# Second attention of a two-layer gated block: the negative maxima leave VectorE as four columns and come back as one row that TensorE reads with a stride

## The chip, the cores and the metric

The kernel runs on one core of a Trainium2 chip. The metric is the device time of one execution in microseconds (us). Engines are named as in the profile: PE is TensorE (PEld its weight loads), DVE VectorE, ACT ScalarE, POOL GpSimd, SP SyncE, which here issues the DMAs. The program is written instruction by instruction: each engine has a queue that it works through in order, and semaphores tie the queues together.

## The reference, cut to what matters

Two layers, each a gated cross attention on a context of 1601 tokens and a gated feed-forward part. The change lies in the second layer's attention:

```python
q = (text_hidden @ Wq).reshape(B, T_text, 16, 128)...      # B = 4, T_text = 256
k = (vision_tokens @ Wk).reshape(B, T_vis, 8, 128)...      # T_vis = 1601
scores = jnp.einsum('bhtd,bhsd->bhts', q, k) / scale
scores = jnp.where(mask, scores, -jnp.inf)
attn = jax.nn.softmax(scores, axis=-1)
out = jnp.einsum('bhts,bhsd->bhtd', attn, v)
return out.transpose(0, 2, 1, 3).reshape(B, T_text, 2048) @ Wo
```

Softmax needs, for each query and head, a number near the maximum of its scores, to be subtracted before the exponential.

## The kernel before, in words

A planner (class `Plan`) writes out lists of pieces: `plan.main` for the first layer and the second attention (`stage0` to `stage2`), `plan.ffn` for the last feed-forward part. Each engine's function (`tensor_main`, `vector_main`, `scalar_main`, `gpsimd_main`, `sync_main`) goes over the same list and issues its share of each piece, so the list sets the order of every queue. What runs at once is decided by the distance between pieces in the list and by the waits.

The second attention (`stage2`) works on 32 groups g: 4 batches by 8 pairs of heads. A group has 512 query columns (2 heads by 256 queries) in `qh` (high half, bf16) and `ql` (low half). The keys come in 13 tiles of up to 128. Scores are computed transposed, keys on partitions and queries along the row. For a tile s = 13 g + kt the pieces are:
- `s1`: PE makes the scores in bank 0 or 1 with three matmuls of 512 columns. For kt 0 and 1 a fourth one goes first (L1389): it adds the row of negative maxima, `mrw`, to each key's scores; its weights are ones, and of `mrw` only partition 0 is not zero. The scores of the tiles from 2 on are taken against key differences (`dch`), so the row needs to be added to two tiles only, since it then stays in the sum. ACT takes the exponential (L1975).
- `c1`: ACT casts it to bf16 (L1982). `r1`: DVE makes the low half (L1719). POOL adds the tiles up for the denominators (L2115, L2118).
- `v1`, three tiles later: three matmuls with the values, into bank 2 or 3; they wait for `r1` of their tile (`p_low`).

After a group: `o1a` (PE, 4 float32 products of one column into bank 7, once POOL has all sums: `summed1`), DVE L1722 and L1724, POOL L2124 makes a diagonal matrix, `o1b` (PE, float32, bank 7) spreads it, ACT copies it (L1998), `o1c` (DVE L1733) scales the output.

Ahead of a group come its queries (`qp`, 12 matmuls, then `ql`) and its maxima: `md` and `mb` (16 matmuls of 512 or 289 columns into banks 4 to 6, ACT L1993, DVE L1700), then `mf`: DVE reduces 128x8 to `mm1`, 128x4 (L1706): partition n, column u holds the maximum of query 128 u + n. Then the columns must become a row:
- `m1n`: PE transposes `mm1` into bank 7 (L1377), DVE clamps and negates the 4x128 result into `mng` (L1711), which frees bank 7.
- `m1r`: SP writes `mng` to DRAM, 4 rows of 128 (L2231), waits for it, and reads the 512 numbers back into partition 0 of `mrw` (L2236).

In the list three other steps of the maxima's generator lie between `mf` and `m1n`, about two tiles; `m1r(g)` comes after s1(13 g - 9), nine tiles ahead of the group's first scores. Bank 7 is shared: `m1n`, `o1a`, `o1b`, the transposes of the normalisation (`ln3`, L1043), output projections. Each of these waits until the one before it in the list has been emptied (`free[7]`). L722 is a helper through which all matmuls but the transposes go, and L658 is the helper that waits. All SBUF tiles lie in one tensor, so the profile calls them `arena`; the banks are `BK`; `rowd` is the DRAM scratch.

Of the kernel before, what the change touches and what calls it, by code (L numbers as in the profile page):

```python
# [6 lines left out]
BF16 = mybir.dt.bfloat16  # L7
U8 = mybir.dt.uint8
I32 = mybir.dt.int32
ALU = mybir.AluOpType  # L10
# [38 lines left out]
class Plan:  # L49
# [424 lines left out]
    def maxima(self, g):  # L474
        for k in range(9):
            if k < 8:
                self.fill(self.turn(g, 4), "md", g, k // 2, k % 2)
                self.main.append(("md", g, k // 2, k % 2))
                yield
            if k:  # L480
                self.fill(self.turn(g, 5), "mb", g, (k - 1) // 2, (k - 1) % 2)
                self.main.append(("mb", g, (k - 1) // 2, (k - 1) % 2))
                yield
        self.main.append(("mf", g))
        yield
        yield
        yield
        self.fill(7, "m1n", g)
        self.main.append(("m1n", g))
        yield  # L490
        self.rowed.add(g)
        self.main.append(("m1r", g))
        yield

    def stage2(self):
# [7 lines left out]
            to.append(p)  # L503

        def masked(b):
            assert b < 2 or ("m1n", 8 * (b - 1) - 1) in self.slot
            assert ("m1n", 8 * b) not in self.slot
            for k in range(7):
                piece("mk", b, k)
                yield  # L510
# [161 lines left out]
def program(nc, a, out):  # L672
    root = ExitStack()
    with root:
# [5 lines left out]
        def sem(name):  # L680
            return root.enter_context(nc.semaphore(name))
# [39 lines left out]
        def mm(out_, lhsT, rhs, start=True, stop=True):  # L721
            return T.matmul(out_, lhsT, rhs, start=start, stop=stop, skip_group_check=True)  # L722
# [129 lines left out]
        on1 = sb("on1", [128, 128], F32, CTb)  # L852
        ones = sb("ones", [128, 128], F32, CTb)
        dn = sb("dn", [128, 8], F32, CTb)
        mng = sb("mng", [4, 2, 128], BF16, CTb)
        Ph = [sb(f"Ph_{i}", [128, 512], BF16, (L1, CTb)[i == 0]) for i in range(NR)]
        Pl = [sb(f"Pl_{i}", [128, 512], BF16, (L1, SM)[i == 0]) for i in range(NR)]
        ckf = sb("ckf", [128, NKT, 128], F32, L1)
# [231 lines left out]
        def pool_mask(b, k):  # L1090
            if k == 6:
# [4 lines left out]
                for lo, hi in ((0, 401), (401, HALF)):  # L1096
# [11 lines left out]
        mcb_done, q_high, max1_done, p_high, p_low, summed1, pv_done, diag_done, ck_high, ck_low, tern_done = (  # L1108
            sem(n) for n in ("mcb_done", "q_high", "max1_done", "p_high", "p_low", "summed1", "pv_done",
                             "diag_done", "ck_high", "ck_low", "tern_done"))  # L1110
        l1_set, t_lt, t_half, dn_recip, pv_taken = (sem(n) for n in ("l1_set", "t_lt", "t_half", "dn_recip", "pv_taken"))

        def prep_over(queue):
# [13 lines left out]
        def tensor_main():  # L1127
            for piece in plan.main:
# [238 lines left out]
                elif kind in ("md", "mb"):  # L1367
# [3 lines left out]
                    pe.wait_ge(mx_ready, g // 8 + 1)  # L1371
                    mm(BK[i][:, 0:hi - lo], qh[:, g % 3, 128 * u:128 * u + 128],
                       (cmd if kind == "md" else cmb)[:, g // 8 % 2, lo:hi]).then_inc(full[i], 1)
                elif kind == "m1n":
                    g, = arg
                    pe.wait_ge(max1_done, g + 1)
                    T.transpose(BK[7][0:4, 0:128], mm1[:, :], idn[:, :]).then_inc(full[7], 1)  # L1377
                elif kind == "s1":
                    s, = arg
                    g, kt = s // NKT, s % NKT  # L1380
                    b, r, m = g // 8, g % 3, rows_of(kt)[0]
                    ks = slice(128 * kt, 128 * kt + m)
                    high = cth[:, b, ks] if kt < 2 else dch[b][:, 128 * kt - 256:128 * kt - 256 + m]
                    o = BK[i][0:m, :]
                    pe.wait_ge(*emptied("qp", g))
                    if kt < 2:
                        pe.wait_ge(rows1[g % 2], 16 * (g // 2 + 1))
                        pe.wait_ge(l1_set, 4)
                        mm(o, onb[:, 0:m], mrw[:, g % 2, :], stop=False)  # L1389
                    mm(o, high, qh[:, r, :], start=False, stop=False)  # L1390
                    mm(o, high, ql[:, r, :], start=False, stop=False)
                    mm(o, ctl[:, b, ks], qh[:, r, :], start=False).then_inc(full[i], 1)
                elif kind == "v1":
                    s, = arg
                    g, kt = s // NKT, s % NKT
                    b, k, m = g // 8, s % NR, rows_of(kt)[0]
                    j = 2 + g % 2
                    pe.wait_ge(p_low, s + 1)
                    pe.wait_ge(ck_low, 3 * b + 3)
                    if kt == 0:  # L1400
                        pe.wait_ge(pv_taken, g - 1)
                    mm(BK[j][:, :], ckh[0:m, b, kt, :], Ph[k][0:m, :], start=(kt == 0), stop=False)
                    mm(BK[j][:, :], ckl[0:m, b, kt, :], Ph[k][0:m, :], start=False, stop=False)
                    mm(BK[j][:, :], ckh[0:m, b, kt, :], Pl[k][0:m, :], start=False,
                       stop=(kt == NKT - 1)).then_inc(pv_done, 1)
                elif kind == "o1a":
                    g, = arg
                    pe.wait_ge(summed1, 12 * (g + 1))
                    pe.wait_ge(l1_set, 4)
                    for u in range(4):  # L1410
                        t = mm(BK[7][:, u:u + 1], acc[:, g % 2, 128 * u:128 * u + 128], ones[:, 0:1])
                    t.then_inc(full[7], 1)
                elif kind == "o1b":
                    g, = arg
                    pe.wait_ge(diag_done, g + 1)
                    mm(BK[7][:, :], ones[:, :], dg[:, :, :].rearrange("p u n -> p (u n)")).then_inc(full[7], 1)
                elif kind == "o1h":
                    t2, = arg
                    i, n = slot["o1p", B - 1, t2]
                    pe.wait_ge(free[i], n)  # L1420
                    pe.wait_ge(pv_taken, 8 * B - 1)
                    project1(i, t2, 0, H - 2)
                elif kind == "o1p":
                    b, t2 = arg
                    pe.wait_ge(pv_taken, 8 * b + 8)
                    project1(i, t2, H - 2 if b == B - 1 else 0, H).then_inc(full[i], 1)
                elif kind == "twc":
                    k, = arg
                    pe.wait_ge(t_half, 3 * k + 1)
                    mm(BK[7][:, 0:1], on1[:, :], asum[:, k:k + 1]).then_inc(full[7], 1)  # L1430
# [13 lines left out]
        def vector_main():  # L1444
# [10 lines left out]
            for piece in plan.main:  # L1455
# [247 lines left out]
                elif kind == "mf":  # L1703
                    g, = arg
                    dve.wait_ge(*emptied("mb", g, 3, 1))
                    V.tensor_reduce(mm1[:, :], mp1[:, :, :], AX.X, ALU.max).then_inc(max1_done, 1)  # L1706
                elif kind == "m1n":
                    g, = arg
                    dve.wait_ge(full[7], n + 1)
                    dve.wait_ge(bounced1[g % 2], 16 * (g // 2))  # L1710
                    V.tensor_scalar(mng[:, g % 2, :], BK[7][0:4, 0:128], -1e20, -1.0, ALU.max, ALU.mult).then_inc(free[7], 1)  # L1711
                elif kind == "r1":
                    s, = arg
                    k, m = s % NR, rows_of(s % NKT)[0]
# [419 lines left out]
        def sync_main():  # L2134
# [13 lines left out]
            for piece in plan.main:  # L2148
# [77 lines left out]
                elif kind == "m1r":  # L2226
                    g, = arg
                    k = g % 2
                    sp.wait_ge(*emptied("m1n", g))
                    sp.wait_ge(rows1[k], 16 * (g // 2))  # L2230
                    SP.dma_start(rowd[k][0:4, :], mng[:, k, :]).then_inc(bounced1[k], 16)  # L2231
                    sp.wait_ge(bounced1[k], 16 * (g // 2 + 1))
                    sp.wait_ge(l1_set, 4)
                    if g >= 2:
# [243 lines left out]
```

## Time and profile before

| | |
|---|---|
| median of 3 runs | 1621.13 us (1619.86 to 1626.16) |
| the profiled execution's own time | 1623.28 us |
| its span | 1622.0 us |
| second attention, from the first transpose of maxima to the last group | about 684 to 1560 us |
| busy over the whole span | PE 87%, DVE 76%, ACT 68%, POOL 50% |

The span is what the profile covers; the execution's time is 1.28 us longer. Busy shares are means over stages that are limited differently, so the chain of waits and the idle time ahead of single instructions are what tells where a removed instruction or wait counts. The busy time of matmuls is modelled at their ends, so the spacing of starts is the better measure of what one costs in a dense stretch. "PEclk" is the granted clock of TensorE as a share of 2.4 GHz.

### The profile page before, as it was taken

Reading aid. Unit: us, or ns where it says so; the run is one execution under the profiler, and the core shown is the slowest. Engines: PE = TensorE matmul, PEld = TensorE weight load, DVE = VectorE, ACT = ScalarE, POOL = GpSimd, SP = SyncE. Lnnn points to the kernel's source line nnn. Section 1 sums busy time; section 2 is a strip of 40 time slices with the busy share of each in tenths; the row PEclk is TensorE's granted clock in tenths of the full one; section 3 lists DMA queues with packets and bytes.
Section 4 is the critical chain, followed back from the end, with each engine's and each line's share of the span. In section 5 each row is a group of like instructions: output and inputs, shape, how many; then the busy total and the mean of one; then the engine's idle time right before and its main releaser. Section 6 shows DMA issues by size and latency. Waiting matters only on the chain.

```text
span 1622.0 us, 25718 instructions
## 1 busy us (share of the span) xinstructions
PE 1412.5 (87%) x8502; PEld 695.3 (43%) x8588; DVE 1233.2 (76%) x2247; ACT 1104.4 (68%) x2028; POOL 805.2 (50%) x664
## 2 busy tenths in 40 slices
PE   5788788888888888788899988899988999899999
PEld 3243243343333343244455544445543446454455
DVE  6667667767786256688999586979689997899857
ACT  4657656756755755487788586778587876787844
POOL 4014013014040022178778468687497875587843
PEclk9798998999988999899999999999999999999999
DMA  4001200300340100100000000000010000000000
GB/s 159 1 1 38 46 2 1 62 2 1 63 183 1 53 1 6 36 27 6 1 1 1 21 1 26 1 2 21 1 27 27 1 27 1 27 1 1 1 1 27
DMA packets 20491, 36.72 MB, mean 23 GB/s; under 512 B 4898, under 2 KB 15238, under 8 KB 19334
## 3 DMA queue, kind: packets, MB, share of 16 engines
q1 hardware_dynamic: 20358, 35.07, 7.4%
q8 instruction: 69, 1.13, 0.3%
q14 instruction: 64, 0.52, 0.1%
HBM read 26.53 MB, written 1.15 MB: 17 GB/s over the span
## 4 chain that ended last, share of the span: by engine, by line
PE 32%; DVE 9%; issue 7%; POOL 7%; ACT 4%; DVEq 0%; ACTq 0%; POOLq 0%
PE BK L722 32%; DVE arena L1719 4%; POOL arena L2118 4%; DVE arena L1700 2%; ACT arena L1982 1%; ACT arena L1975 1%; POOL arena L2124 1%; POOL arena L2115 1%; ACT arena L1993 1%; ACT L1975 0%; DVE arena L2307 0%; POOL arena L2103 0%; POOL arena L2092 0%; DVE arena L1071 0%; DVE arena L2313 0%
## 5 line engine op out<-in xcount | busy, mean ns | idle before, releaser
L722 PE MATMUL BK<-arena 128*128 128x512 bf16 (+11 forms) x8172 | 1366.5, 367 | 174.1 <-DVE arena L1537 39.3
L722 PEld LDWEIGHTS BK<-arena 128*128 128x128 bf16 (+6 forms) x8258 | 659.0, 111 | 852.0 <-issue 213.9
L2118 POOL TENSOR_TENSOR arena<-arena 128x512 f32<-128x512 f32 (+1 forms) x352 | 506.2, 1438 | 155.1 <-ACT arena L1975 132.9
L1719 DVE TENSOR_TENSOR arena<-arena 128x512 bf16<-128x512 f32 (+1 forms) x416 | 498.4, 1206 | 31.6 <-ACT arena L1982 30.4
L1975 ACT ACTIVATE arena<-BK,arena 128x512 f32<-128x512 f32 (+1 forms) x416 | 286.8, 689 | 128.7 <-PE BK L722 112.8
L1873 ACT ACTIVATE arena<-BK 128x512 f32<-128x512 f32 (+1 forms) x416 | 227.3, 604 | 92.7 <-PE BK L722 87.1
L1537 DVE TENSOR_REDUCE arena<-BK 128x1 f32<-128x512 f32 x384 | 244.5, 684 | 59.7 <-PE BK L722 58.6
L1982 ACT CAST arena<-arena 128x512 bf16<-128x512 f32 (+1 forms) x416 | 254.1, 611 | 0.0
L1700 DVE CUSTOM_DVE_ANT_0 arena<-BK,arena 128x512 bf16<-128x512 f32 (+1 forms) x256 | 145.1, 567 | 40.1 <-PE BK L722 39.8
L1993 ACT ACTIVATE arena<-BK 128x512 bf16<-128x512 f32 (+1 forms) x256 | 130.9, 512 | 58.1 <-PE BK L722 56.8
L2029 POOL TENSOR_TENSOR arena<-arena 128x256 f32<-128x256 f32 (+6 forms) x45 | 30.2, 671 | 186.4 <-ACT arena L1810 184.1
L2115 POOL TENSOR_TENSOR arena<-arena 128x512 f32<-128x512 f32 x32 | 45.7, 1430 | 65.0 <-ACT arena L1975 65.0
L2056 POOL TENSOR_TENSOR arena<-arena 128x512 bf16<-128x512 f32 x24 | 28.2, 1173 | 98.6 <-ACT arena L1839 79.6
L1664 DVE TENSOR_TENSOR arena<-BK,arena 128x512 f32<-128x512 f32 x32 | 22.0, 688 | 46.7 <-ACT arena L1929 46.6
L2124 POOL TENSOR_TENSOR arena<-arena 128x512 f32<-128x512 f32 x32 | 47.5, 1484 | 10.5 <-DVE arena L1724 10.5
L1793 ACT COPY arena<-BK 128x256 f32<-128x256 f32 (+1 forms) x52 | 18.9, 372 | 48.0 <-DVE arena L1483 48.0
L1483 DVE TENSOR_TENSOR arena<-BK,arena 128x256 f32<-128x256 f32 (+1 forms) x56 | 23.5, 422 | 36.1 <-PE BK L722 36.1
L2073 POOL CAST arena<-arena 128x256 bf16<-128x256 f32 x16 | 6.4, 398 | 82.2 <-ACT arena L1913 82.2
L2040 POOL TENSOR_TENSOR arena<-arena 128x1024 f32<-128x1024 f32 (+2 forms) x15 | 23.4, 1593 | 29.2 <-DVE arena L974 29.2
L1739 DVE SCALAR_TENSOR_TENSOR arena<-BK,arena 128x256 f32<-128x256 f32 x8 | 3.9, 483 | 42.5 <-PE BK L722 42.5
L1998 ACT COPY arena<-BK 128x512 f32<-128x512 f32 x32 | 18.8, 587 | 25.2 <-PE BK L722 25.2
L2103 POOL TENSOR_TENSOR arena<-arena 128x384 bf16<-128x384 f32 (+1 forms) x20 | 19.9, 1015 | 23.2 <-ACT arena L1953 23.2
(179 smaller groups left out, 876.3 us busy)
## 6 DMA issues: line engine op xcount, KB each, us to landing
arena<-arena SPq DMA_DIRECT2D x144, 50.0 KB, 2.2
arena<-in_ctxT SPq DMA_DIRECT2D x8, 800.5 KB, 4.5
arena<-in_ctxk SPq DMA_DIRECT2D x4, 768.0 KB
arena<-in_wo SPq DMA_DIRECT2D x1, 2048.0 KB, 7.4
arena<-in_wqT SPq DMA_DIRECT2D x1, 2048.0 KB, 7.5
arena<-in_x SPq DMA_DIRECT2D x4, 256.0 KB, 9.8
arena<-in_rsel SPq DMA_DIRECT2D x1, 1024.0 KB, 9.4
arena<-in_rw1T SPq DMA_DIRECT2D x1, 1024.0 KB, 5.2
```

The source lines that it names most:

```text
L722: return T.matmul(out_, lhsT, rhs, start=start, stop=stop, skip_group_check=True)
L1537: V.tensor_reduce(mxp[:, g % 2, u, c:c + 1], BK[i][:, :], AX.X, ALU.max).then_inc(free[i], 1)
L1700: V.tensor_tensor_reduce(out=junk[:, 0:w], in0=BK[i][:, 0:w], in1=rl[:, k % 3, 0:w], scale=1.0, scalar=-3e38, op0=ALU.add, op1=ALU.max, ac ...
L1719: V.tensor_tensor(Pl[k][0:m, :], P1[k][0:m, :], Ph[k][0:m, :], ALU.subtract).then_inc(p_low, 1)
L1873: A.activation(P0[(2 * s + r) % NP][0:m, :], BK[i][0:m, :], ACT.Exp, scale=0.25).then_inc(free[i], 1)
L1975: A.activation(P1[k][0:m, :], BK[i][0:m, :], ACT.Exp, scale=SCALE1, bias=mcb[0:m, b, kt:kt + 1]).then_inc(free[i], 1)
L1982: A.copy(Ph[k][0:m, :], P1[k][0:m, :]).then_inc(p_high, 1)
L1993: A.activation(rl[:, k % 3, 0:w], BK[i][:, 0:w], ACT.Relu).then_inc(free[i], 1)
L2029: G.tensor_tensor(sv[:, :, 0:w], sv[:, :, 0:w], sv[:, :, w:2 * w], ALU.add).then_inc(pool_chain.sem, pool_chain.up())
L2115: G.tensor_tensor(acc[:, g % 2, :], P1[(s - 1) % NR][:, :], P1[k][:, :], ALU.add).then_inc(summed1, 1)
L2118: G.tensor_tensor(acc[0:m, g % 2, :], acc[0:m, g % 2, :], P1[k][0:m, :], ALU.add).then_inc(summed1, 1)
L2124: G.tensor_tensor(dg[:, :, :], idn[:, :].unsqueeze(1).to_broadcast([128, 4, 128]), dn[:, 4:8].unsqueeze(2).to_broadcast([128, 4, 128]), AL ...
```

## The change

The transpose is gone. DVE clamps and negates `mm1` where it lies, right behind the reduction, in piece `mf`; `mng` is now 128 partitions of 4 numbers. The piece `m1n` no longer exists, though the generator yields as often as before, so all other pieces keep their places. A new semaphore, `max1_neg`, tells SP. The store to DRAM moves 128 pieces of 4 bf16 numbers (8 bytes) where it moved 4 of 256 bytes, and number 4 n + u of the DRAM row is now query 128 u + n. It is read back as it lies, so the matmul that adds the row (64 of them, two in each group) reads `mrw` in steps of 4 elements, 8 bytes: 128 elements from offset 0, 128 from offset 1, and so on.

```diff
@@ Plan.maxima
-        self.fill(7, "m1n", g)
-        self.main.append(("m1n", g))
         yield
         self.rowed.add(g)
         self.main.append(("m1r", g))
@@
-        mng = sb("mng", [4, 2, 128], BF16, CTb)
+        mng = sb("mng", [128, 2, 4], BF16, CTb)
@@ tensor_main
-                elif kind == "m1n":
-                    g, = arg
-                    pe.wait_ge(max1_done, g + 1)
-                    T.transpose(BK[7][0:4, 0:128], mm1[:, :], idn[:, :]).then_inc(full[7], 1)
@@ s1
-                        mm(o, onb[:, 0:m], mrw[:, g % 2, :], stop=False)
+                        mm(o, onb[:, 0:m], mrw[:, g % 2, :].rearrange("p (n u) -> p u n", u=4), stop=False)
@@ vector_main
                     V.tensor_reduce(mm1[:, :], mp1[:, :, :], AX.X, ALU.max).then_inc(max1_done, 1)
-                elif kind == "m1n":
-                    g, = arg
-                    dve.wait_ge(full[7], n + 1)
+                    dve.wait_ge(max1_done, g + 1)
                     dve.wait_ge(bounced1[g % 2], 16 * (g // 2))
-                    V.tensor_scalar(mng[:, g % 2, :], BK[7][0:4, 0:128], -1e20, -1.0, ALU.max, ALU.mult).then_inc(free[7], 1)
+                    V.tensor_scalar(mng[:, g % 2, :], mm1[:, :], -1e20, -1.0, ALU.max, ALU.mult).then_inc(max1_neg, 1)
@@ sync_main, m1r
-                    sp.wait_ge(*emptied("m1n", g))
+                    sp.wait_ge(max1_neg, g + 1)
                     sp.wait_ge(rows1[k], 16 * (g // 2))
-                    SP.dma_start(rowd[k][0:4, :], mng[:, k, :]).then_inc(bounced1[k], 16)
+                    SP.dma_start(rowd[k][0:4, :].rearrange("a (b u) -> (a b) u", u=4), mng[:, k, :]).then_inc(bounced1[k], 16)
                     sp.wait_ge(bounced1[k], 16 * (g // 2 + 1))
```

On PE, around the transpose of group 13, this stands in the queue before (the matmuls of 512 columns that wait for `p_low` are `v1`, those that wait for free0 or free1 are `s1`, the 256-column ones `qp`, and the one-column ones `o1a` of group 11):

```order
L722 MATMUL BK<-arena 128x512 [waits free0]
L722 MATMUL BK<-arena 128x512 x2
L1377 MATMUL BK<-arena 4x128 [waits max1_done,free7]
L722 MATMUL BK<-arena 128x512 [waits p_low]
L722 MATMUL BK<-arena 128x512 x2
L722 MATMUL BK<-arena 128x512 [waits free1]
L722 MATMUL BK<-arena 128x512 x2
L722 MATMUL BK<-arena 128x256 [waits free4]
L722 MATMUL BK<-arena 128x256 x11
L722 MATMUL BK<-arena 128x1 [waits summed1,free7]
L722 MATMUL BK<-arena 128x1 x3
L722 MATMUL BK<-arena 128x512 [waits p_low]
```

And this stands at the same place now:

```order
L720 MATMUL BK<-arena 128x512 [waits free0]
L720 MATMUL BK<-arena 128x512 x2
L720 MATMUL BK<-arena 128x512 [waits p_low]
L720 MATMUL BK<-arena 128x512 x2
L720 MATMUL BK<-arena 128x512 [waits free1]
L720 MATMUL BK<-arena 128x512 x2
L720 MATMUL BK<-arena 128x256 [waits free4]
L720 MATMUL BK<-arena 128x256 x11
L720 MATMUL BK<-arena 128x1 [waits summed1,free7]
L720 MATMUL BK<-arena 128x1 x3
L720 MATMUL BK<-arena 128x512 [waits p_low]
```

Only the transpose has gone; but `free7` at `o1a` now stands for an earlier user of bank 7, no longer for the transpose that DVE must have read.

On DVE, for the same group, before (L1719 is `r1`, L1071 to L1079 are the mask of the next batch, L1722 is `o1a`):

```order
L1706 TENSOR_REDUCE arena<-arena 128x4 [waits free5]
L1719 TENSOR_TENSOR arena<-arena 128x512 [waits pv_done,p_high]
L1071 TENSOR_SCALAR arena<-arena 128x1601
L1073 TENSOR_TENSOR arena<-arena 128x2 [waits dve_own]
L1075 TENSOR_SCALAR arena<-arena 128x1 [waits dve_own]
L1077 RECIPROCAL arena<-arena 128x1 [waits dve_own]
L1079 SCALAR_TENSOR_TENSOR arena<-arena 128x1 [waits dve_own]
L1719 TENSOR_TENSOR arena<-arena 128x512 [waits pv_done,p_high]
L1711 TENSOR_SCALAR arena<-BK 4x128 [waits bounced11,full7]
L1719 TENSOR_TENSOR arena<-arena 128x512 [waits pv_done,p_high]
L1722 TENSOR_SCALAR arena<-BK 128x4 [waits full7]
```

Now the clamp stands right behind the reduction (all line numbers are lower by some):

```order
L1701 TENSOR_REDUCE arena<-arena 128x4 [waits free5]
L1704 TENSOR_SCALAR arena<-arena 128x4 [waits bounced11,max1_done]
L1712 TENSOR_TENSOR arena<-arena 128x512 [waits pv_done,p_high]
L1069 TENSOR_SCALAR arena<-arena 128x1601
L1071 TENSOR_TENSOR arena<-arena 128x2 [waits dve_own]
L1073 TENSOR_SCALAR arena<-arena 128x1 [waits dve_own]
L1075 RECIPROCAL arena<-arena 128x1 [waits dve_own]
L1077 SCALAR_TENSOR_TENSOR arena<-arena 128x1 [waits dve_own]
L1712 TENSOR_TENSOR arena<-arena 128x512 [waits pv_done,p_high] x2
L1715 TENSOR_SCALAR arena<-BK 128x4 [waits full7]
```

The clamp moved up over two `r1` (and here over the mask's five instructions), and waits for the reduction on its own engine where it waited for PE. On SP the order of the DMAs is as before.

## Rows read from the trace of the kernel before

**Rows 1.** The page's busy times and its chain by engine.

```profile
PE 1412.5 (87%) x8502; PEld 695.3 (43%) x8588; DVE 1233.2 (76%) x2247; ACT 1104.4 (68%) x2028; POOL 805.2 (50%) x664
...
PE 32%; DVE 9%; issue 7%; POOL 7%; ACT 4%; DVEq 0%; ACTq 0%; POOLq 0%
```

**Rows 2.** Busy time by stretch: us, PE, PEld, DVE, ACT, POOL, PEclk, DMA, GB/s.

```profile
1068.00:1134.00 66.00, 65.39 (x317) 32.44 (x323) 57.90 (x98) 54.61 (x100) 50.20 (x37) 0.97 0.04 13
683.00:1550.00 867.00, 791.70 (x3876) 404.11 (x3948) 738.77 (x1233) 655.17 (x1176) 635.32 (x457) 0.99 0.04 11
```

**Rows 3.** Chain in order of time, pieces on PE's transpose: start, us, what (15 such).

```profile
684.25 0.37 PE BK L1377
...
1495.10 0.11 PE BK L1377
```

**Rows 4.** Timeline of PE around transposes, of a dense stretch and behind it.

```profile
1109.91 0.27 PE L1377 MATMUL BK<-arena 128*4 128x128 f32 x1
1110.10 23.14 PE L722 MATMUL BK<-arena 128*128 128x512 bf16 x116
...
1133.07 0.27 PE L1377 MATMUL BK<-arena 128*4 128x128 f32 x1
...
1173.01 0.27 PE L1377 MATMUL BK<-arena 128*4 128x128 f32 x1
```

**Rows 5.** Timeline of PE, its idle time that ends with DVE L1711 (10 such rows).

```profile
809.15 8.01 PE L722 MATMUL BK<-arena 128*128 128x1 f32 x38 [0.71 <-DVE arena L1711]
...
945.83 0.66 PE L1043 MATMUL BK<-arena 128*128 128x128 f32 x4 [1.05 <-DVE arena L1711]
...
1259.49 3.88 PE L722 MATMUL BK<-arena 128*128 128x1 f32 x20 [0.51 <-DVE arena L1711]
...
1397.35 0.66 PE L1043 MATMUL BK<-arena 128*128 128x128 f32 x4 [2.46 <-DVE arena L1711]
```

**Rows 6.** Timeline of all engines around the longest of them.

```profile
1029.96 0.16 DVE L1706 TENSOR_REDUCE arena<-arena 128x4 f32<-128x8 f32 x1
...
1036.28 0.27 DVE L1711 TENSOR_SCALAR arena<-BK 4x128 bf16<-4x128 f32 x1
...
1036.61 1.08 PE L722 MATMUL BK<-arena 128*128 128x1 f32 x8 [2.55 <-DVE arena L1711]
...
1037.72 0.16 DVE L1722 TENSOR_SCALAR arena<-BK 128x4 f32<-128x4 f32 x1 [0.57 <-PE BK L722]
...
1037.92 0.18 DVE L1724 RECIPROCAL arena<-arena 128x4 f32<-128x4 f32 x1
...
1037.93 4.24 PE L722 MATMUL BK<-arena 128*128 128x512 bf16 x12 [0.24 <-issue]
```

**Rows 7.** Busy time by stretch, behind two of the stalls (columns as in Rows 2).

```profile
1037.00:1041.00 4.00, 3.76 (x14) 1.79 (x16) 2.83 (x6) 0.69 (x2) 1.41 (x1) 0.57 0.00 1
1041.00:1044.00 3.00, 3.00 (x14) 1.38 (x13) 2.14 (x2) 2.52 (x5) 2.52 (x2) 1.00 0.00 0
945.00:949.00 4.00, 3.12 (x26) 2.68 (x28) 2.20 (x3) 3.10 (x6) 2.44 (x3) 1.00 0.00 1
```

**Rows 8.** Chain in order of time, pieces on DVE L1711 (8 such).

```profile
1308.31 0.21 DVE arena L1711
```

**Rows 9.** Groups of instructions by form, 680 to 1550 us: count, busy us and mean ns.

```profile
L722 PE MATMUL BK<-arena 128*128 128x512 bf16 x2522 | 610.6, 382 | 46.8 <-DVE arena L1719 35.0 <-ACT arena L1975 4.9 <-ACT arena L1993 1.3
...
L722 PE MATMUL BK<-arena 128*128 128x512 f32 x62 | 34.2, 635 | 16.3 <-POOL arena L2124 16.3
```

**Rows 10.** DMA issues: two on SP in time; two small ones, KB, us to landing.

```profile
1111.94 0.24 SPq L2231 DMA_DIRECT2D rowd<-arena  x1
...
1113.08 0.21 SPq L2236 DMA_DIRECT2D arena<-rowd  x1
...
rowd<-arena SPq DMA_DIRECT2D x16, 4.0 KB, 1.4
...
arena<-in_mcol SPq DMA_DIRECT2D x1, 6.0 KB, 4.2
```

More of the change, by code:

```diff
@@ L505, in masked @@
         def masked(b):
-            assert b < 2 or ("m1n", 8 * (b - 1) - 1) in self.slot
-            assert ("m1n", 8 * b) not in self.slot
+            assert b < 2 or 8 * (b - 1) - 1 in self.rowed
+            assert 8 * b not in self.rowed
             for k in range(7):
@@ L1110, in program @@
                              "diag_done", "ck_high", "ck_low", "tern_done"))
+        max1_neg = sem("max1_neg")
         l1_set, t_lt, t_half, dn_recip, pv_taken = (sem(n) for n in ("l1_set", "t_lt", "t_half", "dn_recip", "pv_taken"))
```

## The prediction

> **What bounds the kernel now.** I read the page first. Over the whole span PE is busy 87% and is the largest part of the chain that ended last, but a third only, with DVE and POOL behind it [rows 1]; the reader is to see that no engine is the bound throughout. So I went to the stage of the change. From 683 to 1550 us PE is busy 792 of 867 us and DVE 739 [rows 2]. In a dense stretch such as 1068 to 1134 us PE is busy 65.4 of 66 us: there a group takes 23.16 us, one transpose to the next, and every PE instruction counts. The next group takes 39.9 us [rows 4]; the mean of the stage is 867/32 = 27 us, and in the slower groups the chain runs over DVE or POOL for long pieces. A PE instruction is therefore worth its time only where the chain passes through it; for the transpose that is so 15 times of 32 [rows 3].
>
> Then I looked for the idle time of PE that the removed instructions end. There are ten such places, of 0.40 to 2.55 us [rows 5, 6]. Their cause is in the order, not in the transpose's own length: bank 7, which the next piece needs (`o1a` seven times, a normalisation's transpose three times), is freed by DVE L1711, and L1711 stands on DVE behind an `r1` (L1719). When DVE is late, PE stands before a bank although it has work that needs nothing of it. Eight of these ten are on the chain [rows 8]; those at 1259 and 1520 us are not, where POOL leads.
>
> **What is removed on PE.** 32 transposes. In the dense stretch the next matmul starts 0.19 us after the transpose [rows 4], so one costs about 0.2 us of PE, 6.4 us in all, and on the chain 15 x 0.2 = 3.0 us. The other 17 fall into time in which PE would wait anyway.
>
> **What the freed bank gives.** After the stall, PE did the blocked piece (1.08 us for `o1a` [rows 6], 0.66 us for the normalisation's four transposes [rows 5]) and then `v1`, which needs the `r1` that stood just ahead of L1711. Without L1711 the blocked piece runs inside the stall, and PE then waits for the end of that `r1`, which lies 0.27 + 0.04 us before the old release. So each place on the chain gives the smaller of its stall and 0.31 us plus the piece: 0.71 twice (809 us and one like it), 0.97 for the normalisation's three (stalls 1.05, 1.05, 2.46), 0.51 twice (like that at 1259 us), and 1.39 for the stall of 2.55. That is 1.42 + 2.91 + 1.02 + 1.39 = 6.7 us.
>
> The longest place has something on top. PE stood 2.55 us, and behind it the granted clock was 0.57 over 4 us, mostly the lower level of 1.2 GHz, and 2.4 GHz (1.00) after that [rows 7]; the twelve matmuls from 1037.93 took 4.24 us [rows 6]. At full clock 116 starts take 22.97 us (1110.10 to 1133.07 [rows 4]), 0.20 us each with shorter ones among them, so 0.21 for one of 512 columns and 2.5 us for twelve. With `o1a` run inside it, the wait shrinks to some 1.2 us. Behind the idle of 1.05 us at 945.83 PE kept its full clock [rows 7], so I take the loss as gone: 1.7 us. If it is not, that term is nothing.
>
> **DVE.** L1711 took 0.27 us on 4x128 from PSUM. The new instruction is 128x4 from SBUF, nearest to L1722, 128x4 from PSUM, 0.16 us [rows 6]. Its wait for the reduction on its own engine is like that of L1724 behind L1722, which starts 0.04 us after its end [rows 6]. I bound the pair with its wait between 0.04 us more than L1711 alone (0.31) and, as that is the smallest row here, 0.07 us less (0.16 + 0.04); taken: the latter, 2.2 us of DVE time, of which a tenth or so is on the chain, 0.2 us. It now delays the `r1` behind the reduction by 0.2 us, and spares the one behind the old place 0.27 us, so nothing is late next.
>
> **The DMAs.** SP issues the read of the row 1.14 us after the write [rows 10]; that is the write's whole way. The new write has 128 pieces of 8 bytes instead of 4 of 256. Bounds: the same 1.1 us, or 4.2 us as the small load over 128 partitions, 3.1 us more. The write of the first layer's maxima, 16 pieces, lands in 1.4 us [rows 10], and the queues are as good as idle, so I take some 1.5 us. What hides it: `m1r(g)` stands nine tiles before the group's first scores, and a tile takes 23.1/13 = 1.8 us, so 16 us are there even in the dense stretch. SP's queue has DMAs of context and mask behind it, needed later still. The clamp's earlier place (at 1030.2 and no longer 1036.3 [rows 6]) adds cover. Only group 0 has no nine tiles: its chain goes reduction, transpose, clamp, two DMAs. Its transpose is on the chain with 0.37 us [rows 3] and is counted; at the upper bound this one place would lose about 2 us. Taken: 0.
>
> **The strided read.** 64 matmuls read the same 512 columns of the same type, with a step of 8 bytes. No row shows a strided moving operand. It can't be faster than contiguous, so the lower bound is 0. The upper bound I take from the nearest slower reading, the float32 product of 512 columns: 34.2 us for 31 products, 1.10 us each, against 610.6/2522 = 0.24 us [rows 9]; 0.86 us more, 55 us over 64 matmuls. The row it is nearest to is the bf16 one, which differs in nothing but the step; taken: 0.
>
> The Trainium skill, "SBUF — State Buffer", section "Door 1: The DMA port swizzle", has a note on lines of 16 bytes. It says two or more hits in a line reach full bandwidth, by which a step of 8 bytes costs nothing; the same note says that each access that crosses to a new line pays a penalty, and this read crosses at every second element where the contiguous one crosses at every eighth. By the first half the sum stands; by the second it is the rival below. No run here shows which.
>
> **The sum.** 3.0 + 6.7 + 1.7 + 0.2 + 0 + 0 = 11.6 us on the chain of before. It is not all kept: a chain that lay just behind takes over. DVE is busy 85% and POOL 73% of the stage [rows 2], and every place where PE was held by DVE's lateness is one where DVE is the next bound, since v1 and the exponentials go on depending on it. I keep two thirds: 8 us. Against the profiled execution's own 1623.3 us this gives 1615.3; that execution is 2.2 us above the median of 1621.1, so for a median 1613.
>
> **Rivals.**
> - *The strided read runs at half rate.* A length more, 0.21 us, 64 x 0.21 = 13.4 us of PE. By the share of the transposes, 15 of 32 are on the chain, and a little more as PE gets longer: 7 us. It eats the gain: 1620. For it: nothing in the trace speaks against it, and the second half of the note; against it: the first half.
> - *The strided read runs at a quarter rate or worse, and the kernel is slower.* Three lengths more, 0.63 us per matmul, 40 us of PE; at this size PE becomes the bound in more groups, and I take 0.6 of it, 24 us, less the gain of 8: 1637. The point from which this mechanism makes the kernel slower by more than 8 us is (8 + 8)/(64 x 0.6) = 0.4 us per matmul, about three times its length. For it: float32 products are four to five times as long as bf16 ones [rows 9]. Against it: those do more passes; this one has the same columns.
> - *The stalls move and nothing is gained.* PE gets past bank 7 and waits for the same DVE `r1` at `v1`; chains of POOL and DVE take back all but the transposes in the dense groups: 3 us kept at most, 1618 to 1621. For it: the two idle places off the chain, and groups that POOL leads. Against it: in the dense groups nothing is close behind PE.
> - *The new DMA is late.* It would have to take 16 us, except for group 0; 2 us there, and a median of 1615. The trace gives it little.
>
> **How the numbers follow.** A run of this kernel can tell a change of about 0.5%, 8.1 us. Forecast, read free and gain between 4 and 16 us: 0.50, of it 0.33 faster and 0.17 within 0.5%. Stalls moved: 0.17, all within (0.02 of it faster). Half rate: 0.17, of it 0.14 within and 0.03 slower. Quarter rate or worse: 0.13, slower. DMA late or another loss: 0.03, within 0.02 and slower 0.01. Together: faster 0.35, within 0.48, slower 0.17. The range starts at 1604, the whole sum and a restored phase besides (1621 - 17), and ends at 1630, half rate with no gain kept; the quarter rate is left out with a little at the low end. The likeliest case alone: 1605 to 1617.
>
> **What would show it.** In the profile after: no idle time of PE ends with the clamp, `o1a` starts right behind `qp`, and the stall of 2.55 us is about half as long, with the clock at 1.00 behind it. In dense groups the spacing from group to group falls from 23.16 to about 22.96 us; if it rises to 23.4, the read is at half rate, and beyond 24 at a quarter. The matmuls of PE should be 32 fewer with busy time lower by some 8 us. The clamp should take 0.16 us. The time from the write's issue to the read's should stay under 3 us, and no idle time of PE should end with a DMA. The forecast is wrong if the exponentials of tiles 0 and 1 come late in every group, or if the new idle time of PE ahead of L1719 equals what went from L1711.

## The result, and the profile after

The changed kernel is a little slower: median 1632.04 us (1624.34 to 1636.31, 15 runs) against 1626.02 us (1617.82 to 1633.74, 15 runs) before, ratio 1.0037, 95% interval 1.0019 to 1.0054, so some 6 us. I had forecast 1613 and a range to 1630. That forecast was worked out from a median of 1621.13 us over three runs of the kernel before; over fifteen it is 1626.02 us, so 5 of the 19 us by which the forecast missed lie in its base. The profiled execution took 1632.33 us.

The page of the kernel after, busy times, against [rows 1]:

```profile
PE 1430.7 (88%) x8470; PEld 693.9 (43%) x8556; DVE 1249.5 (77%) x2247; ACT 1104.6 (68%) x2028; POOL 806.0 (49%) x664
```

PE has 32 matmuls fewer, as the change says, and is busy 18 us more; DVE has as many instructions and is busy 16 us more. Both went up where I expected both to fall.

Where most of the 18 us of PE are is seen at the tiles whose matmuls read the row. Here are the starts of ACT's exponentials, one for each tile (start, duration, and the idle time before with what ended it), for the last tile of a group (65 keys) and tiles 0 and 1 of the next, in a dense stretch. First before (only the tiles, what ACT does between them left out):

```profile
1102.18 0.69 ACT L1975 ACTIVATE arena<-BK,arena 65x512 f32<-65x512 f32 x1
...
1104.13 0.69 ACT L1975 ACTIVATE arena<-BK,arena 128x512 f32<-128x512 f32 x1 [0.26 <-PE BK L722]
...
1105.76 0.69 ACT L1975 ACTIVATE arena<-BK,arena 128x512 f32<-128x512 f32 x1 [0.44 <-PE BK L722]
```

Then after, cut in the same way:

```profile
1105.54 0.68 ACT L1968 ACTIVATE arena<-BK,arena 65x512 f32<-65x512 f32 x1
...
1107.72 0.69 ACT L1968 ACTIVATE arena<-BK,arena 128x512 f32<-128x512 f32 x1 [0.49 <-PE BK L720]
...
1109.59 0.69 ACT L1968 ACTIVATE arena<-BK,arena 128x512 f32<-128x512 f32 x1 [0.68 <-PE BK L720]
```

The distances were 1.95 and 1.63 us and are 2.18 and 1.87 us: 0.23 and 0.24 us more for each of the two tiles whose matmul reads with a step, and ACT's idle time before them grew by that. All other distances of the group stayed within 0.03 us, but for the one at the clamp (below). A dense group went from 23.15 to 23.71 us.

The read itself can be seen on PE. In windows so narrow that a row holds a single matmul, the timeline of PE after shows the one that reads the row for tile 0, and the next:

```profile
1106.42 0.61 PE L720 MATMUL BK<-arena 128*128 128x512 bf16 x1
1106.85 0.40 PE L720 MATMUL BK<-arena 128*128 128x512 bf16 x1
```

The next one starts 0.43 us later. Where the same row is read without a step (e1 below), the same two start at 1106.84 and 1107.06 us, 0.22 us apart. The third matmul follows the second after 0.24 us, 0.02 us more than the usual 0.22, which makes 0.23 us in all.

The clamp, which I put at 0.16 us, in the view by source line (ns, min/median/max):

```profile
L1704 DVE TENSOR_SCALAR arena<-arena x32: 171/548/2324, 684.2 to 1525.8; 128x4 bf16<-128x4 f32 x32
```

And two of its 32 places, the usual one and the longest, in the timeline of DVE and of POOL:

```profile
1089.10 0.55 DVE L1704 TENSOR_SCALAR arena<-arena 128x4 bf16<-128x4 f32 x1
...
1202.14 2.32 DVE L1704 TENSOR_SCALAR arena<-arena 128x4 bf16<-128x4 f32 x1
```

```profile
1088.28 1.34 POOL L2111 TENSOR_TENSOR arena<-arena 128x512 f32<-128x512 f32 x1 [0.34 <-ACT arena L1968]
...
1202.66 1.77 POOL L2096 TENSOR_TENSOR arena<-arena 128x384 bf16<-128x384 f32 x2
```

POOL's instruction ends at 1089.62 and the clamp at 1089.65; POOL's pair ends at 1204.43 and the clamp at 1204.46. It is so in 30 of the 32 places: the clamp ends 0.02 to 0.04 us after one of POOL's instructions. At 904.37 us, with POOL idle, it takes 0.17 us. The last place, at 974.94 us, takes 0.17 us with POOL busy, and fits too: POOL's instruction there (973.94 us, 1.07 us long) ends at 975.01, and the clamp could not have ended before 975.11 by its own length. In 29 of the 30 places it is the instruction that POOL is running when the clamp starts. In the longest it is not: the one that was running ended at 1202.70, and the clamp let POOL's next two pass as well. This repeats in e1 and e4 (2.30 us at 753.39 and at 744.99 us, 2.31 and 2.29 us near 1200 us), and I have no account of it.

What was right in the forecast is also there. No idle time of PE ends with the clamp any more, so those ten places [rows 5] are gone. But the longest of them, which stood at 1036.61 with 2.55 us [rows 6], now reads, in the timeline of PE and in the stretch behind it (columns as in rows 2):

```profile
1042.46 5.73 PE L720 MATMUL BK<-arena 128*128 128x512 bf16 x16 [1.80 <-DVE arena L1712]
```

```profile
1044.00:1048.00 4.00, 4.00 (x11) 1.69 (x10) 3.40 (x4) 2.63 (x5) 3.22 (x3) 0.64 0.00 0
```

PE now waits for the `r1` (L1712) that DVE has late, and the granted clock falls behind it as before [rows 7]: 0.64 here, the lower level for most of it. The write of the row now lands after 2.9 us (2.5 to 3.8 over the 32, view by source line), and at group 0 the row arrives late for the first tile (timeline of PE):

```profile
690.89 6.15 PE L720 MATMUL BK<-arena 128*128 128x512 bf16 x19 [2.41 <-DMA arena<-rowd]
```

### The profile page after: what moved, and what is told of

Read it like the earlier page. It is cut to its first block, busy times and chain, and to the rows that moved or that the text cites. A ratio compares the mean times of both kernels' runs of the same rounds, so it can differ in the third digit from the quotient of the medians.

```text
span 1631.0 us, 25621 instructions
## 1 busy us (share of the span) xinstructions
PE 1430.7 (88%) x8470; PEld 693.9 (43%) x8556; DVE 1249.5 (77%) x2247; ACT 1104.6 (68%) x2028; POOL 806.0 (49%) x664
## 4 chain that ended last, share of the span: by engine, by line
PE 33%; DVE 10%; issue 7%; POOL 5%; ACT 3%; DMA 0%; DVEq 0%; ACTq 0%; POOLq 0%
PE BK L720 33%; DVE arena L1712 6%; POOL arena L2111 3%; DVE arena L1695 2%; ACT arena L1975 1%; POOL arena L2117 1%; ACT arena L1968 1%; POOL arena L2108 1%; ACT L1968 0%; DVE arena L2300 0%; DVE arena L1685 0%; POOL arena L2085 0%; ACT arena L1986 0%; DVE arena L1069 0%; DVE arena L2306 0%
## 5 line engine op out<-in xcount | busy, mean ns | idle before, releaser
L720 PE MATMUL BK<-arena 128*128 128x512 bf16 (+11 forms) x8172 | 1386.3, 372 | 169.6 <-DVE arena L1712 44.9
L1712 DVE TENSOR_TENSOR arena<-arena 128x512 bf16<-128x512 f32 (+1 forms) x416 | 500.7, 1219 | 26.1 <-ACT arena L1975 25.5
L2033 POOL TENSOR_TENSOR arena<-arena 128x1024 f32<-128x1024 f32 (+2 forms) x15 | 23.4, 1590 | 29.4 <-DVE arena L972 29.4
L1991 ACT COPY arena<-BK 128x512 f32<-128x512 f32 x32 | 18.7, 586 | 19.8 <-PE BK L720 19.8
```

Source lines behind the costliest of these rows:

```text
L1712: V.tensor_tensor(Pl[k][0:m, :], P1[k][0:m, :], Ph[k][0:m, :], ALU.subtract).then_inc(p_low, 1)
```

## The experiments

Ratios are to the kernel before, on the same chip, with 95% intervals. "Dense group" is the distance of two reductions `mf` in the dense stretches, eight or nine of them in a run, which lie within 0.03 to 0.07 us of each other, so that the table's values hold to 0.01 or 0.02 us; "stage" is from the reduction of group 0 to that of group 31, in one profiled execution (before 833.0 us, after 841.6 us).

| run | ratio | dense group, us | stage, us |
|---|---|---|---|
| before | 1 | 23.15 | 833.0 |
| after | 1.0037 (1.0019 to 1.0054) | 23.71 | 841.6 |
| e1, row read without a step | 0.9983 (0.9958 to 1.0007) | 23.22 | 830.0 |
| e2, before with the step alone | 1.0051 (1.0030 to 1.0072) | 23.64 | 842.8 |
| e3, transpose and clamp left out | 0.9975 (0.9951 to 0.9999) | 23.15 | 827.6 |
| e4, step on the weight loads | 0.9984 (0.9961 to 1.0007) | 23.24 | 834.7 |
| e5, a reduction for the clamp | 1.0025 (1.0008 to 1.0042) | 23.65 | 835.3 |
| e6, e4 with one reduction | 0.9989 (0.9971 to 1.0008) | 23.18 | 831.5 |
| e7, small DMA pieces alone | 1.0000 (0.9985 to 1.0014) | 23.18 | 833.8 |
| e8, group 0 without its wait | 1.0046 (1.0029 to 1.0062) | 23.71 | 842.8 |

The stage of single executions scatters by a few us from one to the next, as some groups outside the dense stretches fall one way or another; the dense group does not, and carries more.

**e1, the row read without a step.**

```diff
-  mm(o, onb[:, 0:m], mrw[:, g % 2, :].rearrange("p (n u) -> p u n", u=4), stop=False)
+  mm(o, onb[:, 0:m], mrw[:, g % 2, :], stop=False)
```

> The changed kernel with the row read without a step. The row then stands in the wrong order: each query's scores are shifted by another query's maximum. Theory 1 (the strided read costs the time): a dense group took 23.72 us after and 23.16 us before, with 0.2 us of transpose gone, so two strided reads cost 0.76 us, 0.38 each. Here the dense group falls to about 22.95 us, PE's busy time for the bf16 products falls by some 18 us, and the kernel is 10 to 16 us faster than the changed one, 0.3 to 0.6% below before. Theory 2 (the clamp on DVE, 0.55 us where I took 0.16, is the cause): the dense group stays above 23.5 us and the kernel above before.

Measured: 0.9983, dense group 23.22 us, 0.49 us under that of the changed kernel, 0.25 us for each read. Against the changed kernel that is 1.0037/0.9983 = 1.0054, some 9 us. The strided read is more than the whole loss. But the dense group did not fall to 22.95, and the gain that is left, 0.17%, can't be told from none.

**e2, the step alone, in the kernel before.** The same line, the other way round, with nothing else changed.

> The kernel before with the strided read alone; transpose, clamp and DMAs as before, so the row is again in the wrong order. Theory 1: dense group 23.16 + 0.76 = 23.9 us, 10 to 16 us slower than before, ratio 1.006 to 1.010. Theory 2: as before within 3 us.

Measured: 1.0051, some 8 us. The dense group is 23.64 us, 0.49 more, not 0.76: my expectation had added 0.2 us for a transpose that, as e3 shows, was not there to be gained, and had put the clamp's 0.07 us (e5) on the read.

**e3, transpose and clamp left out.** Of the computation the maxima are missing.

```diff
-  self.fill(7, "m1n", g)
-  self.main.append(("m1n", g))
+  G.memset(mng[:, :, :], 0.0).then_inc(l1_set, 1)     # once
-  sp.wait_ge(*emptied("m1n", g))
+  sp.wait_ge(max1_done, g + 1)
```

> The kernel before with transpose and clamp left out: the row of zeros travels by the same DMAs and is read without a step. This is the whole of what the freed bank and the missing transposes can give. My sum said 11.6 us on the old chain, two thirds kept: 8 us, ratio 0.995, dense group 22.95 us. The rival that the stalls only move gives 3 us or less, ratio 0.998 or more.

Measured: 0.9975, some 4 us (0.2 to 8 by the interval): half of what I had kept and a third of the sum. The dense group is 23.15 us, unchanged. In the trace the exponentials of a dense group start at the same distance from the reduction as before, to 0.01 us. The chain around the transpose of group 16, before (its reduction starts at 1108.77 us) and here (1102.79 us; start, us, what):

```profile
1107.91 2.16 PE BK L722 x10
1110.07 0.11 PE BK L1377
```

```profile
1101.95 2.16 PE BK L720 x10
...
1104.11 7.90 PE BK L720 x44
```

The chain of before went through the transpose, and that was all that it showed: the time without it is the same. The row that I should have looked at is the weight load behind the transpose, before and then here:

```profile
1110.09 0.98 PEld L722 LDWEIGHTS BK<-arena 128*128 128x128 bf16 x6 [0.31 <-DVE arena L1719]
```

```profile
1104.11 0.98 PEld L720 LDWEIGHTS BK<-arena 128*128 128x128 bf16 x6 [0.49 <-DVE arena L1717]
```

The next matmul, `v1`, waits for an `r1` of DVE, and it is this wait that ends its idle time; the transpose stood in a gap that stays. Without the transpose the weight load only waits longer, 0.49 in place of 0.31 us, and both start 1.32 us after their reduction. The stage is 5.4 us shorter, all of it in slower groups. At the three former stalls of 1.05, 1.05 and 2.46 us [rows 5] the normalisation's transposes start without a wait. The one at 1036 us has become:

```profile
1031.06 5.53 PE L720 MATMUL BK<-arena 128*128 128x512 bf16 x15 [1.57 <-DVE arena L1717]
```

```profile
1031.00:1034.00 3.00, 2.94 (x8) 1.12 (x9) 2.96 (x7) 0.51 (x1) 1.41 (x1) 0.58 0.00 0
```

A third shorter, and the clock falls all the same, to 0.58 over the 3 us behind it.

**e4, the step on the weight loads of the maxima.** The row comes back in order and nothing of the computation is missing.

```diff
-  mm(BK[i][:, 0:hi - lo], qh[:, g % 3, 128 * u:128 * u + 128],
+  mm(BK[i][:, 0:hi - lo], qh[:, g % 3, :].rearrange("p (n u) -> p u n", u=4)[:, u, :],
-  mm(o, onb[:, 0:m], mrw[:, g % 2, :].rearrange("p (n u) -> p u n", u=4), stop=False)
+  mm(o, onb[:, 0:m], mrw[:, g % 2, :], stop=False)
```

> The changed kernel with the step moved from the row's read to the weight loads of the maxima: partition n of column u now holds query 4 n + u, so the row comes back in order and is read without a step. 16 weight loads in each group read 128 columns in steps of 4. If weight loads with a step are as slow as the strided read (0.38 us for 512 columns, so about 0.1 us for 128) and hidden behind matmuls as other loads, it is like the run with the contiguous read, 10 to 16 us faster than the changed kernel. If they are not hidden, 16 x 0.1 = 1.6 us in each group, 30 us or more slower.

Measured: 0.9984, dense group 23.24 us, within 0.02 us of e1. 16 weight loads of 128 columns in steps of 4 cost nothing that shows, and it is not that they got long and were hidden: the 204 bf16 weight loads of 128 columns in two dense groups, the 32 strided ones among them, are busy 20.3 us, against 19.8 us in e1; two matmuls of 512 columns with that step cost 0.49 us.

**e5, a second reduction in the place of the clamp.** The clamp at -1e20 is left out, and the ones are -1.

```diff
-  V.tensor_scalar(mng[:, g % 2, :], mm1[:, :], -1e20, -1.0, ALU.max, ALU.mult).then_inc(max1_neg, 1)
+  V.tensor_reduce(mng[:, g % 2, :], mm1[:, :].unsqueeze(2), AX.X, ALU.max).then_inc(max1_neg, 1)
```

> The changed kernel, but the second small DVE instruction is again a reduction (128x4 over a last axis of one) in place of the clamp, and the ones that carry the row are -1 (the clamp at -1e20 is left out). Place, operands, wait and semaphores are those of the clamp. If the clamp's 0.55 us is a wait for a port that GpSimd holds, as I think, since reductions took 0.16 us everywhere, this one takes 0.16 to 0.20 us in all 32 places, the dense group falls by the 0.07 us by which e2's 23.65 and the changed kernel's 23.72 us differ, and the kernel is 1 to 3 us faster than the changed one. If the 0.55 us comes from the wait on the instruction just before on its own engine, it stays 0.55 us and nothing changes.

Measured: the instruction takes 0.16 us in all 32 places (view by source line):

```profile
L1704 DVE TENSOR_REDUCE arena<-arena x32: 156/157/158, 684.5 to 1519.8; 128x4 bf16<-128x4 f32 x32
```

Same place, same operands, same wait for the instruction before: so it is not the wait on its own engine that makes 0.55 us. The kind of instruction decides, and with the ends that fall together with POOL's that points to something which the clamp shares with POOL. The dense group is 0.06 us shorter than in the changed kernel. The ratio, 1.0025 against 1.0037, points to 2 us, but the intervals overlap.

**e6, e4 with one instruction.** The reduction writes bf16 into the four columns, the ones are -1, and there is no clamp. It is the version that the experiments point to.

```diff
-  V.tensor_reduce(mm1[:, :], mp1[:, :, :], AX.X, ALU.max).then_inc(max1_done, 1)
-  V.tensor_scalar(mng[:, g % 2, :], mm1[:, :], -1e20, -1.0, ALU.max, ALU.mult).then_inc(max1_neg, 1)
+  V.tensor_reduce(mng[:, g % 2, :], mp1[:, :, :], AX.X, ALU.max).then_inc(max1_done, 1)
```

> The version of e4 (step on the weight loads, row read without a step) with one DVE instruction instead of two: the reduction writes bf16 straight into the four columns, the ones are -1, no clamp. If the clamp costs the 0.08 us by which e4's dense group (23.23) stands above the one with nothing in its place (23.15), this one comes to 23.15 us, and the time to that of the run with transpose and clamp left out, ratio 0.997 to 0.998. If the DMA of 128 pieces is what costs, the ratio stays at 0.9984.

Measured: 0.9989, dense group 23.18 us. It beats the changed kernel by some 8 us (1.0037/0.9989 = 1.0048). That it beats the one before is not shown, its interval reaches over 1. And it leaves out the clamp at -1e20, so it is not yet a replacement.

**e7, the small pieces of the DMA alone, in the kernel before.** The row holds ones in place of the maxima.

```diff
-  SP.dma_start(rowd[k][0:4, :], mng[:, k, :])
+  SP.dma_start(rowd[k][0:4, :].rearrange("a (b u) -> (a b) u", u=4), onb[:, 0:4])
```

> The kernel before, whose store to DRAM takes 128 pieces of 8 bytes from a constant tile in place of 4 of 256 (the row is then one everywhere, transposes and clamp still run). Way from issue to the read's issue 2.9 us instead of 1.14. If the slow store matters only for group 0, the distance from group 0 to 1 rises from 11.8 to about 14.2 us, as in the changed kernel, all dense groups stay at 23.16, and the time is 1 to 3 us above before, ratio 1.001 to 1.002. If the small pieces disturb more, dense groups are longer too.

Measured: 1.0000, with the write landing after 2.9 us (2.6 to 3.4) in each group. Group 0 to 1 takes 14.1 us where it took 11.8, as in the changed kernel (14.2), and the dense groups are within 0.03 us of before. The 2.4 us of group 0 are nearly made up for by the end of the stage (833.8 against 833.0 us), at two groups around 1000 us; why there, I can't say.

**e8, the changed kernel, group 0 without its wait.** Tiles 0 and 1 of group 0 read zeros and do not wait; the other groups are as they were.

```diff
-  pe.wait_ge(rows1[g % 2], 16 * (g // 2 + 1))
+  if g:
+      pe.wait_ge(rows1[g % 2], 16 * (g // 2 + 1))
-  mrw[:, g % 2, :]...
+  mrw[:, g % 2 if g else 1, :]...
+  if g == 1:                                # SP, ahead of the row's read
+      sp.wait_ge(*filled("s1", 1))
```

> The changed kernel, in which the first two tiles of group 0 do not wait for the row (they read a row of zeros, so group 0 goes without its maxima). If the exposed DMA of group 0 costs its 2.41 us of PE idle time and the low clock behind it, group 0 to 1 falls from 14.2 to at most 11.8 us and the kernel is 2 to 3 us faster than the changed one, ratio to before 1.002. If the pipeline behind takes it back, ratio 1.0037 as the changed kernel.

Measured: 1.0046, so no gain, though group 0 to 1 fell to 11.3 us. The rival of that expectation holds: what group 0 loses or gains is taken back before the end of the stage (group 3 to 4 alone took 2.2 us longer here than in the changed kernel). With e7 neither side shows the exposed DMA in the result; a cost of up to 2 us would still lie within e7's interval.

**e9 and e10, steps of 2 and of 8 elements** (one execution each, the order of the maxima is wrong). `u=4` in the read becomes `u=2` and `u=8`.

> The changed kernel with the row read in steps of 2 elements (4 bytes) in place of 4; the order of the maxima is wrong again. Read in the trace by the starts of the exponentials: from tile 12 of one group to those of tiles 0 and 1 of the next in a dense stretch, where a strided read of step 4 added 0.23 us each and 0.49 us to a group. If a step costs by the lines of SBUF that it crosses (two or more elements in 16 bytes are free), step 2 is as step 1: dense group 23.22 us; but then step 4 should have been free too. If any step but 1 halves the rate: 23.72 us as after.

> The changed kernel with the row read in steps of 8 elements (16 bytes), wrong order. If the cost grows with the step (each 16-byte line gives one element): double the added cost or more, dense group 24.2 us and above. If any step but 1 halves the rate and no more: 23.72 us.

Measured, the matmul that reads the row for tile 0 and the next one, as above in narrow windows of PE's timeline, first step 2, then step 8:

```profile
1101.04 0.39 PE L720 MATMUL BK<-arena 128*128 128x512 bf16 x1
1101.27 0.38 PE L720 MATMUL BK<-arena 128*128 128x512 bf16 x1
```

```profile
1107.58 1.06 PE L720 MATMUL BK<-arena 128*128 128x512 bf16 x1
1108.46 0.40 PE L720 MATMUL BK<-arena 128*128 128x512 bf16 x1
```

The table has this distance for all four steps, and beside it the distances of the three exponentials (from the last tile of a group to tile 0 of the next, and from tile 0 to 1), all in us:

| step in elements, bytes | exponentials | added to one read | one read, with 0.21 for step 1 | start to next start on PE | dense group |
|---|---|---|---|---|---|
| 1, 2 (e1) | 1.95, 1.63 | 0 | 0.21 | 0.22 | 23.22 |
| 2, 4 (e9) | 1.95, 1.65 | 0.01 | 0.22 | 0.23 | 23.26 |
| 4, 8 (after) | 2.18, 1.87 | 0.24 | 0.45 | 0.43 | 23.71 |
| 8, 16 (e10) | 2.62, 2.32 | 0.68 | 0.89 | 0.88 | 24.61 |

The read is free up to a step of 4 bytes and then its length goes with the step: half rate at 8 bytes, a quarter at 16. All of this is bf16, so whether bytes or elements count is not shown. Of the theories, the one by which any step but 1 halves the rate falls in both runs, and the one by which two elements in 16 bytes are free falls with step 4; that the cost grows with the step (e10) holds.

**e11, each transpose done twice** (one execution), in the kernel before.

```diff
+  T.transpose(BK[7][0:4, 0:128], mm1[:, :], idn[:, :])
   T.transpose(BK[7][0:4, 0:128], mm1[:, :], idn[:, :]).then_inc(full[7], 1)
```

> The kernel before with each transpose done twice. The exponentials of the run without transposes start at the same times, to 0.01 us, as those of before: 23.14 against 23.16 us for a dense group. Theory: the transpose stands ahead of a v1 that waits for its r1 on DVE anyway and is hidden by about its own length. Then a second one sticks out: dense group up by up to 0.2 us, to 23.25 to 23.4 us. If instead there is more room there than one transpose: 23.16 us, unchanged. Time against before: within 5 us either way.

Measured: dense group 23.19 us, 0.03 to 0.04 more for a second transpose. There is room for nearly two of them in the gap that `v1` leaves, and not for one as I thought: the two start 0.11 us apart and `v1` starts 1.35 us after the reduction, where it was 1.33. The single time of 1632.87 us against 1626.79 us is outside the 5 us that I gave; but in its profile the first group begins at 689.6 us where it was 683.9 before, ahead of any changed instruction, and the stage is 3.9 us longer, 1.7 of them at one group outside the dense stretches. From one execution of each I read nothing on the total.

## Why the prediction was wrong, point by point

- **The strided read.** This is the step that failed: "taken: 0". The bounds were right (0 to 0.86 us), the choice inside them was not. It is 0.235 us for each of 64, 15 us of PE, of which 8 to 9 us count (e2: 0.51%; after against e1: 0.54%). The reason given was that the nearest row, the bf16 product, "differs in nothing but the step", and the step is just what costs. The rival "half rate" had 0.21 us and 7 us on the path, and a chance of 0.17. That rival alone gives 1620 and not 1632; 5 of the 12 us are the base (1626.02 in place of 1621.13), the rest is in the next points. My sign for it, the exponentials of tiles 0 and 1 late in every group, came true; the 23.4 us that I gave for a dense group became 23.71, as the 0.2 us of transpose were not gained and the clamp added 0.07. The first half of a note of the Trainium skill ("SBUF — State Buffer", section "Door 1: The DMA port swizzle") stood on the side of my choice: by it two hits in a 16-byte line reach full bandwidth, and a step of 8 bytes has two. The runs differ from it: two hits (8 bytes, the changed kernel) run at half rate, four (4 bytes, e9) at full rate. Here the measurement decides. The second half, that crossing to a new line costs, doesn't fit either as told: step 2 crosses twice as often as step 1 and adds 0.01 us.
- **The transposes, 3.0 us "on the chain".** Worth nothing in the dense groups (e3, e11). The count of 15 places on the chain was right as a reading and wrong as a price: an instruction on the chain can have a second releaser just behind it. Here the idle time of the weight load behind the transpose, ended by L1719, said so. The "0.2 us of PE" for each of the 32 was wrong with it: the next matmul does start 0.19 us after the transpose, but it can start no earlier without it.
- **The freed bank, 6.7 us.** The mechanism was right: the ten stalls went. The term was too large. With the 3.0 us of transposes and 1.7 us of clock it made 11.4, "two thirds kept", and e3 measured 0.25% (0.01 to 0.49%), some 4 us; in its profile the stage is 5.4 us shorter. I had written that DVE takes over, and it does: PE waits 1.57 us for `r1` where it waited 2.55 us for the bank.
- **The clock behind the longest stall, 1.7 us.** Not regained. The stall shrank as forecast ("some 1.2 us", measured 1.57 in e3), and the granted clock still fell to 0.58.
- **The clamp, 0.2 us gained.** Wrong in sign. 0.55 us in place of 0.27, outside the 0.31 us that I gave as its bound. Its nearest row in shape, L1722, reads PSUM, and takes 0.15 to 0.16 us in all 32 places, before and after. It stands ahead of an `r1` that `v1` waits for, and lengthens the dense group by 0.06 to 0.09 us (after against e5, e1 against e3), 2 to 3 us over 32 groups if it were so in all; how much of that is in the time the ratios are too wide to say.
- **The DMA.** The write took 2.9 us and not 1.5, inside my bounds; hidden by nine tiles as computed. At group 0 it cost 2.41 us of PE, the "about 2 us" of the upper bound. Neither shows in the time (e7, e8).
- **The sum as measured.** Strided read + 8 to 9 us, freed bank and transposes - 4, clamp + 1 to 3: + 5 to 8 us, where 6 were measured. Each of the ratios has an interval of some 3 to 4 us either way, so that the sum comes out this close is in part luck.

## What to carry to other kernels

A bf16 matmul's moving operand should be read in steps of at most 2 elements, 4 bytes (e9); if data must be permuted, do it on the weights of a product upstream (e4), where 128 columns in steps of 4 cost nothing here. Before an instruction on the chain is priced, look at what the next instruction on its engine waits for: removing it is worth only the distance to that second releaser. A small DVE instruction that reads and writes SBUF is priced by rows of the same kind of instruction with POOL busy, not by rows of its shape.

## What the runs showed of the hardware that I had not expected

- The time of one read of the moving operand by its step (bf16, 512 columns, dense stretch): 0.21 us at 2 bytes, 0.22 at 4, 0.45 at 8, 0.89 at 16 (e1, e9, after, e10). Weight loads with a step of 8 bytes show no cost beside it (e4: dense group 23.24 against 23.22 us).
- A clamp of 128x4 on DVE from SBUF to SBUF ended 0.02 to 0.04 us after one of POOL's instructions in 30 of 32 places and took up to 2.32 us; a reduction of the same shape in the same place took 0.16 us in all 32. The Trainium skill, "SBUF — State Buffer", section "Who interferes with whom", says that `tensor_scalar` can take a pair of ports that GpSimd uses too, and that the one which is second waits for the other's whole instruction, while `tensor_reduce` on this chip never does. The traces agree in 31 places, with 0.17 us at the one where POOL was idle; at 1202.14 us they differ, as the clamp waited there for two more instructions that POOL began after it.
- The store of 128 pieces of 8 bytes landed after 2.9 us (2.5 to 3.8), where 4 pieces of 256 bytes let the read go after 1.14 us [rows 10].
